# Two of the six gate-times-up products of the first feed-forward stage move from VectorE to ScalarE and GpSimd

## What is computed

```python
xq = fake_quant(c2, clip_x)                                   # one scale for the whole tensor
gate = einsum('bsh,ih->bsi', xq, weight_fake_quant(w_gate))   # i: 704 hidden features
up = einsum('bsh,ih->bsi', xq, weight_fake_quant(w_up))
h = fake_quant(silu(gate) * up, clip_down)                    # one scale: max |silu(gate) * up| over everything
out = einsum('bsi,hi->bsh', h, weight_fake_quant(w_down))
x = x + out
```

## Time and profile before

| | |
|---|---|
| device time, three runs | 1398.55 us median, 1398.45 to 1400.82 |
| the profiled execution | 1398.35 us, of it a span of 1396.6 us |
| PE busy over the span | 1256.0 us, 90% |
| DVE busy | 1039.0 us, 74% |
| ACT busy | 757.2 us, 54% |
| POOL busy | 565.0 us, 40% |
| first-stage products, from first to last matmul | 1274.31 to 1336.25 us |
| PE weight loads of the up products waiting for DVE in 1274 to 1338 us | 19.3 us, 31 times |
| ACT's silu waiting for DVE there | 8.8 us, 15 times |

### The profile page before, as it was taken

How to read it: one execution, slowest core, us unless ns; L and a number is a source line. 1 busy time by engine, 2 the same in 40 slices (tenths; PEclk the granted TensorE clock), 3 DMA queues, 4 the chain that set the end, 5 groups by cost and what they waited for, 6 DMA issues and landing times. The chain is left out here.

```text
span 1396.6 us, 29614 instructions
## 1 busy us (share of the span) xinstructions
PE 1256.0 (90%) x8710; PEld 1000.6 (72%) x8710; DVE 1039.0 (74%) x2792; ACT 757.2 (54%) x1942; POOL 565.0 (40%) x845
## 2 busy tenths in 40 slices
PE   3999999999886699999998999998999999986966
PEld 2768888888765578778777877887887788873323
DVE  5666676667644877787887887877878877886986
ACT  3223333333222567666765766766676677645643
POOL 1443323333322776354444444354453454531114
PEclk8999999999998899999999999999999999997986
DMA  6332122211201700001010000010010000202115
GB/s 231 108 99 77 65 72 106 91 61 61 91 1 53 262 12 2 1 2 32 2 32 3 2 31 2 1 32 3 2 32 1 2 16 2 78 1 65 45 61 180
DMA packets 49993, 70.57 MB, mean 51 GB/s; under 512 B 4466, under 2 KB 42611, under 8 KB 47796
## 3 DMA queue, kind: packets, MB, share of 16 engines
q1 hardware_dynamic: 49284, 68.55, 14.7%
q10 hardware_dynamic: 560, 0.20, 0.1%
HBM read 56.54 MB, written 12.19 MB: 49 GB/s over the span
## 5 line engine op out<-in xcount | busy, mean ns | idle before, releaser
L1082 POOL TENSOR_SCALAR scores<-scores,att_rinv 128x128 f32<-128x128 f32 (+3 forms) x512 | 266.9, 538 | 194.4 <-DVE att_rinv L1303 194.4
L1147 ACT ACTIVATE scores<-scores,att_top 128x128 f32<-128x128 f32 (+3 forms) x512 | 281.6, 553 | 88.6 <-DVE att_top L1285 88.1
L1285 DVE CUSTOM_DVE_ANT_0 scores<-ps_y,w_bias_b,w_null_s 128x128 f32<-128x128 f32 x448 | 229.3, 547 | 78.2 <-PE ps_y L1476 71.3
L301 POOL TENSOR_TENSOR act_w<-act_g,wide_w 128x512 f32<-128x512 f32 x64 | 105.8, 1653 | 283.2 <-DVE act_g L454 268.7
L1155 ACT ACTIVATE keep<-ps_up 128x128 f32<-128x128 f32 (+3 forms) x256 | 112.0, 438 | 167.4 <-PE ps_up L1487 164.1
L1487 PE MATMUL ps_up<-ident,scores 128*128 128x128 f32 x1280 | 191.2, 275 | 10.0 <-DVE keep L1313 9.4
L214 ACT ACTIVATE hid_hi<-hid 128x512 fp32r<-128x512 f32 x80 | 50.5, 632 | 245.2 <-DVE hid L472 245.2
L1487 PEld LDWEIGHTS ps_up<-ident,scores 128*128 128x128 f32 x1280 | 151.4, 141 | 31.2 <-issue 17.1
L1498 PE MATMUL ps_a<-keep,w_val 128*64 128x128 f32 x2560 | 169.1, 279 | 1.3 <-DVE keep L1313 1.3
L1498 PEld LDWEIGHTS ps_a<-keep,w_val 128*64 128x64 f32 x2560 | 138.1, 137 | 22.0 <-issue 20.0
L1564 PE MATMUL ps_gate<-w_wo,o_t 128*128 128x256 f32 x512 | 139.6, 392 | 0.0
(11 more groups left out here) (321 smaller groups left out, 2949.9 us busy)
## 6 DMA issues: line engine op xcount, KB each, us to landing
wide_w<-token_w_dram SPq DMA_DIRECT2D x16, 1024.0 KB, 4.6
x_raw<-in_x_t_dram SPq DMA_DIRECT2D x8, 512.0 KB, 3.8
x_nat<-in_x_nat_dram SPq DMA_DIRECT2D x8, 512.0 KB, 4.7
x_dram<-x_nat SPq DMA_DIRECT2D x8, 512.0 KB, 2.9
w_x1t<-x_dram SPq DMA_DIRECT2D x8, 512.0 KB, 4.1
x_tile<-x_dram SPq DMA_DIRECT2D x8, 512.0 KB, 4.4
out_dram<-res SPq DMA_DIRECT2D x8, 512.0 KB, 3.2
w_bias_b<-in_bias_dram SPq DMA_DIRECT2D x14, 256.0 KB, 4.1
```

Source lines behind the costliest of these rows:

```text
L301: nc.gpsimd.tensor_tensor(act_w[:, k % 2], act_g[:, k % 2], wide_w[:, k], ALU.mult).then_inc(sem.act_w_ready, 1)
L1082: nc.gpsimd.tensor_scalar(s, s, rinv[:, pp, q, hh:hh + 1], 0.0, ALU.mult, ALU.add).then_inc(sem.p_normed, 1)
L1147: nc.scalar.activation(s, s, ACT.Exp, scale=-1.0, bias=top[:, pp, q, hh:hh + 1], accum_out=lsum[:, pp, q, hh:hh + 1]).then_inc(sem.exp_don ...
L1285: dve.tensor_tensor_reduce(scores_of(pp, hh, q), psS[:, hh, 0:n], bias_of(w, h)[:, CAUSAL[q]:CAUSAL[q] + n], 1.0, null_s[:, par, q, h:h + ...
```

## The change

The pieces k = 1 and 3 (`ON_POOL`) are no longer multiplied by VectorE. ScalarE copies their up bank, scaled, out of PSUM into a new tile `up_sb` (`scaled`), and GpSimd multiplies that with the silu into `hid`. TensorE's up bank of these pieces is then free behind ScalarE's copy (`up_odd`). The single counter `ffn_hid` becomes two, `hid_even` and `hid_odd`. ScalarE's `quantise` goes behind the pieces 2 and 4. GpSimd's cast for the next batch stands behind its two products. VectorE keeps four products and all six reductions, those of the pieces 4 and 5 behind the next batch's first product.

```diff
@@ scalar
+                def silus(n, k):
+                    act.wait_ge(sem.fg_done, IC * n + k + 1)
+                    gated(act, n, k - 2)
                     nc.scalar.activation(silu[0:rows(k), k % 2], ps.gate[0:rows(k), k % 2], ACT.Silu,
...
+                def scaled(n, k):
+                    act.wait_ge(sem.fu_done, IC * n + k + 1)
+                    nc.scalar.activation(up_sb[:, k // 2], ps.up[:, 1], ACT.Copy,
+                                         scale=w.in_scale[:, IC + k:IC + k + 1]).then_inc(sem.up_odd, 1)
...
                     for k in range(IC):
-                        silus(IC * n + k, k)
-                        if ahead and k in (1, 2):
-                            quantise(n + 1, k - 1)
+                        silus(n, k)
+                        if k in ON_POOL:
+                            scaled(n, k)
+                        if ahead and k in (2, 4):
+                            quantise(n + 1, k // 2 - 1)
@@ gpsimd
+                def hidden(n, b, k):
+                    pool.wait_ge(sem.silu_ready, IC * n + k + 1)
+                    pool.wait_ge(sem.up_odd, len(ON_POOL) * n + k // 2 + 1)
+                    settle(pool)
+                    nc.gpsimd.tensor_tensor(part(b, k), up_sb[:, k // 2], silu[:, 1], ALU.mult).then_inc(sem.hid_odd, 1)
+
+                def batch(n, b, par, ahead):
+                    for k in ON_POOL:
+                        hidden(n, b, k)
+                    if ahead:
+                        widen(n + 1, par)
@@ vector
+                def batch(n, b, before):
+                    hidden(n, b, 0)
+                    if before is not None:
+                        largest(n - 1, before, 4)
+                        largest(n - 1, before, 5)
+                    hidden(n, b, 2)
+                    largest(n, b, 0)
+                    largest(n, b, 1)
+                    hidden(n, b, 4)
+                    largest(n, b, 2)
+                    hidden(n, b, 5)
+                    largest(n, b, 3)
@@ tensor
+                    if not known(s, 2):
+                        if k - 2 in ON_POOL:
+                            pe.wait_ge(sem.up_odd, len(ON_POOL) * n + k // 2)
+                        else:
+                            pe.wait_ge(sem.hid_odd if k % 2 else sem.hid_even, IC // 2 * n + k // 2)
```

More of the change, by code:

```diff
@@ L1837, in ffn_in_phase, with part, gated @@
         silu = sb("silu", [P, 2, S])
+        up_sb = sb("up_sb", [P, 2, S])
         def rows(k):
             return P if k < IC - 1 else IB
+        def part(b, k):
+            return hid[0:rows(k), k, b] if isinstance(b, int) else hid[0:rows(k), k, bass.ds(b, 1)].squeeze(1)
+        def gated(eng, n, k):
+            if not (known(n, 1) and k < 0):
+                eng.wait_ge(sem.hid_odd if k % 2 else sem.hid_even, IC // 2 * n + k // 2 + 1)
         with nc.Block() as block:
@@ L1916, in hidden @@
                     dve.wait_ge(sem.fu_done, s + 1)
[L1917 to L1920, removed]
+                    last = nc.vector.scalar_tensor_tensor(out=part(b, k), in0=ps.up[0:rows(k), k % 2],
+                                                          scalar=w.in_scale[0:rows(k), IC + k:IC + k + 1],
+                                                          in1=silu[0:rows(k), k % 2], op0=ALU.mult, op1=ALU.mult)
+                    last.then_inc(sem.hid_odd if k % 2 else sem.hid_even, 1)
                 def largest(n, b, k):
                     s = IC * n + k
-                    dve.wait_ge(sem.ffn_hid, s + 1)
+                    gated(dve, n, k)
                     at = slice(s, s + 1) if isinstance(n, int) else bass.ds(s, 1)
                     nc.vector.tensor_reduce(w.hid_max[0:rows(k), at], part(b, k), X, ALU.max, apply_absolute_value=True)
[L1928 to L1933, removed]
+                def batch(n, b, before):
[10 more added lines that the diff above has]
+                    largest(n, b, 3)
                 nc.vector.memset(w.hid_max[:], 0.0)
@@ L1937, in _ @@
                 first_widened()
-                batch(0, B - 1)
-                with dve.Fori(0, B - 1) as b:
-                    batch(b + 1, b)
+                batch(0, B - 1, None)
+                batch(1, 0, B - 1)
+                with dve.Fori(1, B - 1) as b:
+                    batch(b + 1, b, b - 1)
+                largest(B - 1, B - 2, 4)
+                largest(B - 1, B - 2, 5)
                 dve.drain()
@@ L1954, in products @@
                         pe.wait_ge(sem.cq_ready, n + 1)
[L1955 to L1962, removed]
+                    if not known(s, 2):
+                        pe.wait_ge(sem.silu_ready, s - 1)
+                    for c in range(HC):
+                        last = pe.matmul(ps.gate[0:rows(k), k % 2], w.ffn_in[:, 0, c, cols], cq_t[:, par, c],
+                                         start=(c == 0), stop=(c == HC - 1))
+                    last.then_inc(sem.fg_done, 1)
+                    if not known(s, 2):
+                        if k - 2 in ON_POOL:
+                            pe.wait_ge(sem.up_odd, len(ON_POOL) * n + k // 2)
+                        else:
+                            pe.wait_ge(sem.hid_odd if k % 2 else sem.hid_even, IC // 2 * n + k // 2)
+                    for c in range(HC):
+                        last = pe.matmul(ps.up[0:rows(k), k % 2], w.ffn_in[:, 1, c, cols], cq_t[:, par, c],
+                                         start=(c == 0), stop=(c == HC - 1))
+                    last.then_inc(sem.fu_done, 1)
                 def batch(n, par, loads):
@@ L2225, in named_semaphores @@
     sem.silu_ready = new("silu_ready")
-    sem.ffn_hid = new("ffn_hid")
+    sem.hid_even = new("hid_even")
+    sem.hid_odd = new("hid_odd")
+    sem.up_odd = new("up_odd")
     sem.hid_most = new("hid_most")
```

16 lines of the change are left out of this document (6 added, 10 removed).

## The result

The changed kernel takes 1425.28 us (median of four runs, 1422.10 to 1427.88), the kernel before 1398.78 beside it (1398.45 to 1400.82). The ratio is 1.0187, 95% interval 1.0167 to 1.0207: slower by 26.5 us. The prediction was 1423.6 (range 1411 to 1430), slower by 25.3. The profiled execution, the slowest of the four, took 1427.88 us with a span of 1426.1; before it was 1398.35 and 1396.6.

What follows compares the result with a forecast made beforehand. VectorE was taken to bound the stage at 7.50 us a batch. On 1398.35 us, 11.2 for the stage at full clock, 8.8 for the clock and 5.3 for the reload gave 1423.6 us, range 1411 to 1430.

Steps and rivals of the forecast that it cites:

- The ring: First-stage batch: chain from first matmuls through ScalarE's copies and GpSimd's products to the next cast, 9.09 us against 7.50.
- GpSimd's product: GpSimd's multiplication of pieces 1 and 3 in the first stage, taken at 1.29 us from the trace.
- the copy's handover: From the end of ScalarE's copy to GpSimd's product in each batch, 0.22 us.
- the step to silu 3: From GpSimd's product 1 to ScalarE's next silu, no row to read, taken as 0.05 us.
- The contention rival: GpSimd's products slowed to 1.67 us by VectorE, clock falling each time; 1436.2 us, chance 0.10.
- The stage at full clock: First stage's seven batches, first interval and last batch included, longer by 11.2 us.
- The clock: TensorE's idle time of some 2.2 us a batch lowers its clock; four falls of 2.19 us, +8.8.
- The reload: GpSimd's MODIFY_POOL_CONFIG behind the barrier delays the reduction over partitions, +5.3 us on the path.
- The other reload: MODIFY_POOL_CONFIG ahead of the stage's first GpSimd product, 5.64 us, covered by about 8 us of waiting.
- The second stage: Same instructions, costed at nothing; TensorE's clock may shift it by 1 to 2 us either way.
- The sum: Whole kernel: 11.2 + 8.8 + 5.3 = 25.3 us slower.
- VectorE stays the bound: First-stage intervals fall from 7.50 to 6.18 us; 1395.0 us, or 1389.7 without the reload, chance 0.03.

Runs made afterwards that it cites:

- the clock held: Changed kernel with seven more matmuls of 512 columns in each first-stage batch, behind the batch's products, filling TensorE's idle time; 1421.33 us, ratio 1.0167.
- the run with the early reload: Changed kernel with one more one-column partition reduction, result unused, behind GpSimd's last product and ahead of the barrier; 1421.41 us, ratio 1.0166.
- the run with short products: Changed kernel with GpSimd multiplying only 8 of 512 columns of pieces 1 and 3, ScalarE's copy written in place; 1413.30 us, ratio 1.0111.
- pieces 0 and 4: Kernel before with these pieces gated by ScalarE and GpSimd, a tiny GpSimd product at the stage's start, silu 1 ahead of quantising; 1398.20 us, ratio 0.9996.
- late loads: Kernel before with a 128 x 2 GpSimd multiplication behind the last cast, and SyncE's two second-stage loads held until the partition reduction is done; 1404.79 us.
- piece 4 alone: Kernel before with only this piece gated by ScalarE and GpSimd, and an added partition reduction ahead of the barrier; 1402.87 us, ratio 1.0035.

## Why the prediction was right

**The ring.** Predicted 9.09 us at full clock; measured 9.12 and 9.13, and 9.11 to 9.15 with the clock held. Its terms hold singly as well. GpSimd's product took 1.27 for my 1.29 (sixteen, 1.260 to 1.276), the copy's handover 0.23 and 0.24 for 0.22, and the step to silu 3, for which there was no row, 0.10 for 0.05. The Trainium skill's rate (GPSIMD Engine Reference, section 3.1, Elementwise), from which I had estimated 1.12, is 0.15 too low here; going by the trace was right. (By that estimate the sum would have been 8 x 0.34 = 2.7 smaller, not the 2.4 of the prediction.) Two small errors cancel at the ring's end: the cast starts 0.06 us before product 3 is over, and TensorE starts 0.13 behind the cast and not 0.05. The contention rival (1.67) falls: no product was above 1.276. The rule of the Trainium skill (GPSIMD Engine Reference, section 8, Key points) names contention only with VectorE instructions in a two-port mode or with two inputs in SBUF; VectorE's products here have one, and sixteen products agree.

**The stage at full clock.** Predicted +11.2. The first interval is 11.14 (predicted 11.28), but in part by luck: TensorE needed only 1.23 us more than at full clock up to piece 1 (1277.57 to 1280.54, against 1.74), not 2.19, and the reload held GpSimd's first product back by 0.9. With the clock held the six others sum to 54.71 and the last batch takes 10.39 (predicted 10.4). That is 76.24 against 64.95 before: +11.3.

**The clock.** Right in kind, and by chance in number: four falls, in the batches that start at 1297.83, 1317.57, 1328.38 and 1348.11. The term was mis-sized. I had taken 2.19 for each from the first batch, whose first 4.52 us are all at 0.50. Three whole intervals cost 1.49 to 1.69 more than 9.12, and the last batch, at 11.42, 1.03 more than 10.39: the full clock is back before the ring has passed all of TensorE's part (0.52 in the mean from 1297.83 to 1301.00, 1.00 from there to 1308.44). From first matmul to last reduction the changed stage takes 81.96, so the clock's share is 81.96 - 76.24 = 5.7 us, not 8.8. TensorE's idle time was 1.85 to 1.95, not 2.2. One of 1.95 had cost nothing in the experts' phase; here four of seven were followed by a fall, five of seven in the run with the early reload, and none of the seven of 1.61 to 1.79 in the run with short products. The idle time alone does not tell which batch falls.

**The reload.** It is there and on the path, but +7.5, not +5.3. The row on L1138 was read rightly, 5.64 us; it has few transfers beside it, and SyncE's loads at the barrier add 1.9. I costed the DMAs at nothing without asking whether they lengthen a reload. The other reload, ahead of the first product, I called covered by 8 us, at the price of the one ahead of a reduction: it took from 1275.2 until the product at 1283.57, some 0.9 us past copy 1 (done at 1282.44, and 0.22 for the handover). A reload ahead of a TENSOR_TENSOR was never under 6.9 us in the runs.

**The second stage** was given 1 to 2 us either way and took +1.7. Over all runs its length stands near 56.6, 57.7 or 58.4. What picks one of them I did not find out.

**The sum.** 11.3 + 5.7 + 7.5 = 24.5 for 25.3 predicted; two errors, -3.1 and +2.2, nearly cancel, so that the closeness of the sum is partly luck. The rest of the profiled difference is 1.7 in the second stage, 2.9 ahead of the change, and 0.4 at the stage's start, ahead of its first matmul.

**A rival argued wrongly.** "VectorE stays the bound" was to need only products of at most 0.50 us. With products of 0.20 the period was 8.44, for ScalarE's list, with both quantisings moved behind more work, is a ring of its own. I had summed ScalarE's ten instructions to 6.0 us and stopped, and had not followed its list from the batch's first silu to the cast.

## What to carry to other kernels

When work leaves the busiest engine, write down the ring that the next iteration's input closes, engine by engine, before counting what is saved: here 1.3 us of saved VectorE work a batch turned into 1.6 us more, and an order that kept the cast out of the ring took most of that back. The first TENSOR_TENSOR on GpSimd placed between two reductions over partitions costs a reload on each side, 6.9 to 9.0 us ahead of the product and 5.5 to 7.6 ahead of the reduction. Both can be hidden by a tiny instruction of the coming kind placed where GpSimd is waiting anyway, if it waits long enough: with pieces 0 and 4 it did not. TensorE's idle time in the loop had a second price here, in its clock, so look at the granted clock of each interval and not at the mean.

## What the runs showed of the hardware that I had not expected

- A reload's length depends on the instruction behind it and on the transfers beside it. Ahead of a reduction over partitions it took 5.5 us (the added reduction ahead of the barrier) and 5.8 (late loads) with few transfers, and 7.6 with two loads of 512 KB beside it. Ahead of a TENSOR_TENSOR it took 6.97 and 6.95 us with a DMA share of 0.01 and 0.02, 6.9 at a share of 0.28 (piece 4 alone), and 8.1 to 9.0 at the stage's start beside the loads of `c2t`, at a share of about 0.5. So some 1.2 to 2.1 us of it, an estimate from the 6.9, may be these loads'. Holding the loads back was tried for the second stage alone; for the stage's start it is not tested.
- Seven casts between reductions over partitions cause no reload, a TENSOR_TENSOR of two columns does. A cast behind a reduction causes no reload, and the product behind it pays (6.96 us idle by "issue").
- Seven matmuls a batch whose result nobody reads made the stage 5.8 us shorter (85.9 to 80.1), since the clock no longer fell.
